# The last unit of a recurrence: low parts by TensorE and ScalarE, last product by VectorE in halves, output product in two parts

## The chip, the cores and the metric

The kernel runs on one core of one Trainium2 chip. The metric is the time of one execution on the device, in microseconds (us); less is better. The core has five engines that each work through a list of their own: TensorE (PE in the rows; its weight loads are PEld), VectorE (DVE), ScalarE (ACT), GpSimd (POOL) and SyncE (SP, which here issues the DMAs). They wait for each other on semaphores only.

## The reference, cut to what matters

Three layers follow each other: a recurrence over the pixels in two directions, causal attention, and a mixture of long convolutions. Cut to what this case touches:

```python
def _mamba_dir(x, ...):                 # once forward (f), once backward (b); x: 4 x 1024 x 64
    xp, z = split(x @ W_in)             # 128 + 128 channels
    xc = silu(xprev * conv_w[:, 0] + xp * conv_w[:, 1] + conv_b)
    dt_r, Bc, Cc = split(xc @ W_x)      # 8, 16, 16
    dt = softplus(dt_r @ W_dt + b_dt)
    def step(h, inp):                   # h: 128 channels x 16 states
        h = exp(dt_t[:, :, None] * A) * h + (dt_t * x_t)[:, :, None] * B_t[:, None, :]
        return h, einsum('bds,bs->bd', h, C_t)
    y = ys + D * xc
    return (y * silu(z)) @ W_out
y = groupnorm_silu(y_f + y_b) + x       # then a layer norm over the 64 channels, and
q, k, v = x @ Wq.T, x @ Wk.T, x @ Wv.T
out = softmax(causal(q @ k.T * 64 ** -0.5)) @ v
```

## The kernel before, in words

The program is three blocks, one after the other, and all engines meet between two blocks: `mamba_stage` (the recurrence), `attention_stage`, `expert_stage` (the convolutions). `mamba_stage` works through eight **units**: four images times two directions. A tile holds the 128 channels on its partitions and the 1024 pixels of an image along them. For each of the 16 **states** s of a unit:

- ScalarE makes the decay exp(dt * A_s) (`decay_of`, L810; three buffers), a few steps ahead of its use.
- VectorE multiplies dt*x by the row B_s, spread over the partitions (`drive_step`, L1008), and runs the scan h = decay * h + drive over the 1024 pixels (`scan_step`, L1025; four buffers `hidden`). For some states GpSimd (L467) or TensorE (L580) makes the drive instead.
- GpSimd multiplies h by the spread row C_s (L477, four buffers `prod`).
- TensorE adds this product to the sum over the states in PSUM (`ps_y`), a matmul with the identity for each half of 512 pixels (`sum_states`, L589). A 32-bit matmul runs as two records, so a sum is four. The sum of state s stands three states later in TensorE's list (`Y_LAG`).

After the last sum of a unit VectorE multiplies by the gate silu(z) (`gate_of`, L1002), and after both directions TensorE applies W_out (`out_product`, L598, four matmuls, eight records) and ScalarE takes the result out of PSUM with its row sums (`norm_take`, L743).

While a unit runs, the engines also prepare the next one. The eighth and last unit has no next one; in its place it prepares attention for the first image (tables `first_attention` of TensorE and VectorE, `last_unit` of ScalarE, keyed by the state after which a step stands): a layer norm, q, k and v. q and k are each kept as a high part, rounded to a shorter 32-bit format (fp32r), and a low part, the rest. Before the change ScalarE copies the high part out of PSUM (L858, L865) and VectorE subtracts it from PSUM to get the low part (`split_q` L1049, `split_k` L1055). All of these share one PSUM tile, `ps_w`, so each step waits for the one ahead: `keys` for `q_ready`, `values` for `k_ready`.

```python
for k in range(2 * N - Y_LAG, 2 * N):                    # L707, TensorE, after its last state
    sum_states(2 * N * (B - 1) + k, k)
    if k == 2 * N - Y_LAG:
        values()
out_product(B - 1)
...
gate_of(u, 1, B)                                         # L1110, VectorE, after its last scan
take_values()
```

The order on each engine is that in which the code is written; nothing reorders it.

Of the kernel before, what the change touches and what calls it, by code (L numbers as in the profile page):

```python
# [192 lines left out]
TOKEN_NORM = 4  # L193


def mamba_stage(nc, ins, a, g, e, x1):
# [6 lines left out]
    with ExitStack() as ctx:  # L203
# [3 lines left out]
        def sem(name):  # L207
# [31 lines left out]
        minus_ident = sb("minus_ident", [128, 128])  # L239
# [25 lines left out]
            dtx_turned dtx_t_ready drive_t_ready drive_turned tok_psum tok_ready ln_step ln_sq ln_rstd xn_ready  # L265
# [7 lines left out]
         tok_psum, tok_ready, ln_step, ln_sq,  # L273
# [67 lines left out]
        with nc.Block() as block:  # L341
# [81 lines left out]
            def _(pool):  # L423
# [81 lines left out]
            def _(pe):  # L505
# [45 lines left out]
                def add_logarithm(u, i):  # L551

                    pe.wait_ge(minus_one_ready, u)
                    add_part(minus_ident, z_raw)
# [28 lines left out]
                def sum_states(n, k, seeded=None):  # L583
# [7 lines left out]
                    mm.then_inc(prod_summed, 1)  # L591

# [81 lines left out]
                def queries():  # L674
                    pe.wait_ge(a.weights_in, ATTENTION_LOADS)
                    pe.wait_ge(xnt_ready, 1)
# [14 lines left out]
                first_attention = {3: tokens, 7: normed, 10: queries, 12: keys}  # L691
# [15 lines left out]
                for k in range(2 * N - Y_LAG, 2 * N):  # L707
                    sum_states(2 * N * (B - 1) + k, k)
                    if k == 2 * N - Y_LAG:
                        values()  # L710
                out_product(B - 1)

            @block.scalar
            def _(act):
# [24 lines left out]
                def norm_take(b):  # L739
# [3 lines left out]
                    nc.scalar.activation(mixed[:, :], ps_y[0:C, :], ACT.Copy, accum_out=g.sums[:, 0:1]).then_inc(g.mixed_ready, 1)  # L743
# [80 lines left out]
                def square():  # L824
                    act.wait_ge(ln_step, 2)
                    nc.scalar.activation(sq, cen, ACT.Square).then_inc(ln_sq, 1)
# [7 lines left out]
                def last_unit(u, i, s):  # L834
# [21 lines left out]
                    if s == 11:  # L856
                        act.wait_ge(q_psum, 1)
                        nc.scalar.activation(a.q_parts[:, :], ps_w[:, :], ACT.Copy,  # L858
                                             scale=float(C) ** -0.5).then_inc(q_high_ready, 1)
                    if s == 12:  # L860
                        act.wait_ge(q_high_ready, 1)
# [1387 lines left out]
```

## Time and profile before

| | us |
|---|---|
| runs of the kernel | 916.76, 919.76, 920.62 (median 919.76) |
| the profiled execution | 924.74 |
| its span (first to last instruction) | 923.0 |
| TensorE busy | 823.8 (89% of the span) |
| VectorE busy | 676.3 (73%) |
| ScalarE busy | 589.2 (64%) |
| GpSimd busy | 539.8 (58%) |

The granted TensorE clock is 0.957 of full speed over the span. Busy shares are means over three blocks with different limits, so they tell little of a single place; what counts is which wait ends last there. Times in the rows are counted from the start of the span.

### The profile page before, as it was taken

What the parts mean: (1) busy time and instruction counts of PE and PEld (TensorE: products, weight loads), DVE (VectorE), ACT (ScalarE), POOL (GpSimd) and SP (SyncE); (2) the same over time, 40 slices, a digit from 0 to 9 for tenths busy, and PEclk for the clock granted to TensorE, in tenths of its full rate; (3) what the DMA queues carried; (4) which work ended last, traced back from release to release, by engine and by line L of the source; (5) the groups of instructions that cost most, each with busy time, mean ns of one, the idle gap of its engine ahead of it and who ended that gap; (6) DMA issues with size and microseconds to landing.
All of it is one profiled execution on the core that took longest, in us unless ns stands there. A gap on an engine that the chain in (4) does not pass through costs nothing. (4 is left out here: it accounts for less than half of the span.)

```text
span 923.0 us, 10941 instructions
## 1 busy us (share of the span) xinstructions
PE 823.8 (89%) x3234; PEld 506.9 (55%) x3234; DVE 676.3 (73%) x742; ACT 589.2 (64%) x937; POOL 539.8 (58%) x368
## 2 busy tenths in 40 slices
PE   4597999889998898977868899989999999999997
PEld 1343443334443343433334555557888888888886
DVE  3889999998989799899943455646565665565665
ACT  4887779678786878876416456556555554555554
POOL 4788989889898798888846944312212221212220
PEclk8699999979999899998997999999999999999999
DMA  6978795878849688695619600002343443343432
GB/s 149 337 254 312 276 320 211 340 284 271 312 189 366 259 275 307 237 347 196 216 13 157 131 1 1 1 1 76 108 137 100 128 121 108 92 130 98 137 105 77
DMA packets 72470, 165.67 MB, mean 179 GB/s; under 512 B 24194, under 2 KB 25236, under 8 KB 72420
## 3 DMA queue, kind: packets, MB, share of 16 engines
q1 hardware_dynamic: 72436, 165.27, 55.7%
q8 instruction: 15, 0.25, 0.1%
q14 instruction: 19, 0.16, 0.1%
HBM read 162.99 MB, written 2.26 MB: 179 GB/s over the span
## 5 line engine op out<-in xcount | busy, mean ns | idle before, releaser
L477 POOL TENSOR_TENSOR prod<-hidden,c_wide 128x1024 f32<-128x1024 f32 x128 | 300.6, 2360 | 51.6 <-DVE hidden L1025 42.7
L589 PE MATMUL ps_y<-prod,ident 128*128 128x512 f32 x512 | 243.4, 616 | 28.1 <-POOL prod L477 15.0
L1025 DVE TENSOR_TENSOR_SCAN hidden<-decay,ps_d 128x1024 f32<-128x1024 f32 x97 | 221.4, 2282 | 12.6 <-ACT decay L810 3.4
L2061 PE MATMUL ps_conv<-hankel,u_high 128*128 128x512 f32 (+1 forms) x768 | 212.5, 358 | 0.1
L589 PEld LDWEIGHTS ps_y<-prod,ident 128*128 128x128 f32 x512 | 95.3, 194 | 149.0 <-issue 122.6
L2061 PEld LDWEIGHTS ps_conv<-hankel,u_high 128*128 128x128 f32 x768 | 138.5, 189 | 24.7 <-DVE u_t L1924 0.3
L2061 PE MATMUL ps_conv<-hankel,u_low 128*128 128x512 f32 (+1 forms) x384 | 137.2, 357 | 0.0
L1889 POOL CAST block_mix<-even 128x256 fp32r (+1 forms) x32 | 12.7, 398 | 204.6 <-PE sums L1930 204.6
L2178 DVE TENSOR_TENSOR stack<-ps_conv,stack 64x512 fp32r<-64x512 f32 x128 | 88.3, 690 | 60.2 <-ACT stack L2145 57.7
L2178 DVE TENSOR_TENSOR qk<-ps_conv,qk 64x512 fp32r<-64x512 f32 x128 | 88.2, 689 | 48.3 <-ACT qk L2145 45.7
L2145 ACT ACTIVATE stack<-ps_conv 64x512 fp32r<-64x512 f32 x128 | 76.2, 595 | 72.3 <-PE ps_conv L2061 70.4
L2145 ACT ACTIVATE qk<-ps_conv 64x512 fp32r<-64x512 f32 x128 | 76.1, 595 | 61.2 <-PE ps_conv L2061 59.1
L1008 DVE TENSOR_TENSOR ps_d<-ps_x,b_wide 128x1024 f32<-128x1024 f32 x73 | 89.9, 1232 | 10.2 <-DMA b_wide<-bc_rows 5.9
L467 POOL TENSOR_TENSOR drive<-dtx,b_wide 128x1024 f32<-128x1024 f32 x31 | 73.5, 2372 | 19.9 <-DMA b_wide<-bc_rows 19.9
L2061 PEld LDWEIGHTS ps_conv<-hankel,u_low 128*128 128x128 f32 x384 | 72.2, 188 | 12.7
L803 ACT ACTIVATE drive_t<-dtx_t,b_t 128x128 f32<-128x128 f32 x192 | 58.6, 390 | 2.1 <-PE ps_d L580 1.9
L1025 DVE TENSOR_TENSOR_SCAN hidden<-ps_w,drive 128x1024 f32<-128x1024 f32 x24 | 54.6, 2274 | 6.6 <-ACT ps_w L816 6.5
L810 ACT ACTIVATE decay<-dt_b,a_neg_b 128x1024 f32<-128x1024 f32 x49 | 53.7, 1138 | 6.6 <-DVE hidden L1025 6.3
L810 ACT ACTIVATE decay<-dt_f,a_neg_f 128x1024 f32<-128x1024 f32 x48 | 52.3, 1138 | 1.3 <-DVE dt_f L985 0.9
L1610 DVE TENSOR_REDUCE max_parts<-sums 128x1 f32<-128x512 f32 (+1 forms) x48 | 27.5, 599 | 28.2 <-PE sums L1285 18.2
L580 PE MATMUL ps_d<-ident,drive_t 128*128 128x128 f32 x192 | 28.0, 288 | 18.8 <-DVE hidden L1025 14.4
L580 PEld LDWEIGHTS ps_d<-ident,drive_t 128*128 128x128 f32 x192 | 23.0, 147 | 34.6 <-DVE hidden L1025 17.2
(285 smaller groups left out, 1186.7 us busy)
## 6 DMA issues: line engine op xcount, KB each, us to landing
c_wide<-bc_rows SPq DMA_DIRECT2D x128, 512.0 KB, 4.9
b_wide<-bc_rows SPq DMA_DIRECT2D x104, 512.0 KB, 5.8
hankel<-filters SPq DMA_DIRECT2D x32, 1026.0 KB, 5.3
plus<-in_M_phi_plus SPq DMA_DIRECT2D x2, 1024.0 KB, 13.8
minus<-in_M_phi_minus SPq DMA_DIRECT2D x2, 1024.0 KB, 17.4
x_pair<-in_x SPq DMA_DIRECT2D x2, 768.0 KB, 9.2
bc_rows<-mixed_and_low SPq DMA_DIRECT2D x8, 128.0 KB, 5.3
out<-plus SPq DMA_DIRECT2D x8, 128.0 KB, 3.6
```

What stands on the lines that cost most here:

```text
L467: nc.gpsimd.tensor_tensor(drive[DRIVE_OF[s]][:, :], dtx[:, :], b_wide[slot][:, :], ALU.mult).then_inc(share_ready, 1)
L477: nc.gpsimd.tensor_tensor(prod[k % PAIR][:, :], hidden[k % DEEP][:, :], c_wide[s % BC_DEEP][:, :], ALU.mult).then_inc(prod_ready, 1)
L580: mm = nc.tensor.transpose(ps_d[:, t * 128:(t + 1) * 128], drive_t[:, t, :], ident[:, :])
L589: mm = nc.tensor.matmul(out, ident[:, :], halves(prod[k % PAIR])[h], start=False, stop=True, skip_group_check=True)
L803: part = nc.scalar.activation(drive_t[:, t, :], dtx_t[:, t, :], ACT.Copy, scale=b_t[:, t, s:s + 1])
L810: nc.scalar.activation(decay[decay_slot(s, last)][:, :], dt[i][:, :], ACT.Exp, scale=a_neg[i][:, s:s + 1]).then_inc(decay_ready, 1)
L1008: nc.vector.tensor_tensor(ps_d[:, :], ps_x[:, :], b_wide[slot][:, :], ALU.mult).then_inc(drive_ready, 1)
L1025: nc.vector.tensor_tensor_scan(hidden[k % DEEP][:, order], left[:, order], right[:, order], 0.0, ALU.mult, ALU.add).then_inc(hidden_ready, 1)
L1610: nc.vector.tensor_reduce(max_parts[:, i, at // H:at // H + 1], ps_s[c % 2][:, 0:n], AX.X, ALU.max, negate=True).then_inc(part_ready, 1)
L2061: mm = nc.tensor.matmul(out, pairs[q][wp][:, 2 * delta + source, :], rows, start=(delta == 0 and term == 0), stop=(delta == 2 * half + 1 a ...
L2145: nc.scalar.activation(stacks[slot][0:C, source, b, :, half * 2 * HEAD:(half + 1) * 2 * HEAD], ps_conv[source][lanes(b), half, :, :], ACT. ...
L2178: nc.vector.tensor_tensor(low, ps_conv[source][lanes(b), half, :, :], high.bitcast(F32), ALU.subtract).then_inc(conv_low, 1)
```

## The change

In the last unit only, besides two lines of the attention block that follow from it:

- **Low parts.** After `queries` and after `keys` TensorE adds minus the high part to `ps_w` with a matmul by `minus_ident` (`take_away`), and ScalarE copies what is left as the low part. VectorE's `split_q` and `split_k` go. The factor 1/8 of q is put on `wq` once, in the first unit, in place of on each copy of q.
- **v.** `values` stands after state 15 in TensorE's list, and ScalarE takes v out of PSUM in place of VectorE.
- **The last product** (state 15) is made by VectorE in two halves in place of by GpSimd whole; TensorE sums each half for itself, and VectorE gates each half for itself.
- **The output product** goes to `ps_w` in place of `ps_y`, direction f ahead of the sum of state 14, direction b after the gate's halves.

```diff
+                            if last and k == 2 * N - 1:
+                                break
                             pool.wait_ge(hidden_ready, n + 1)
...
+                def last_sum(h):
+                    pe.wait_ge(last_prod, h + 1)
+                    nc.tensor.matmul(halves(ps_y)[h], ident[:, :], halves(prod[(2 * N - 1) % PAIR])[h], start=False,
+                                     stop=True, skip_group_check=True).then_inc(prod_summed, 1)
+
+                def last_out(i):
+
+                    if i == 0:
+                        pe.wait_ge(v_ready, 1)
+                    for h, out in enumerate(halves(ps_w)):
+                        pe.wait_ge(gated_ready, 2 * B - 1 + (h + 1 if i else 0))
+                        mm = nc.tensor.matmul(out[0:C, :], w_out[i], halves(gated[i])[h], start=(i == 0), stop=(i == 1),
+                                              skip_group_check=True)
+                    if i:
+                        mm.then_inc(out_ready, 1)
...
+                def take_away(high, done):
+                    for h, out in enumerate(halves(ps_w)):
+                        mm = nc.tensor.matmul(out, minus_ident[:, :], halves(high)[h], start=False, stop=True,
+                                              skip_group_check=True)
+                    mm.then_inc(done, 1)
+
+                def queries_rest():
+                    pe.wait_ge(q_high_ready, 1)
+                    take_away(a.q_parts, q_psum)
...
+                def keys_rest():
+                    pe.wait_ge(k_high_ready, 1)
+                    take_away(a.k_high, k_psum)
...
-                first_attention = {3: tokens, 7: normed, 10: queries, 12: keys}
+                first_attention = {3: tokens, 7: normed, 10: queries, 11: queries_rest, 12: keys, 13: keys_rest, 15: values}
...
-                for k in range(2 * N - Y_LAG, 2 * N):
+                for k in range(2 * N - Y_LAG, 2 * N - 1):
+                    if k == 2 * N - 2:
+                        last_out(0)
                     sum_states(2 * N * (B - 1) + k, k)
-                    if k == 2 * N - Y_LAG:
-                        values()
-                out_product(B - 1)
+                for h in range(2):
+                    last_sum(h)
+                last_out(1)
...
                     if s == 11:
                         act.wait_ge(q_psum, 1)
-                        nc.scalar.activation(a.q_parts[:, :], ps_w[:, :], ACT.Copy,
-                                             scale=float(C) ** -0.5).then_inc(q_high_ready, 1)
+                        nc.scalar.activation(a.q_parts[:, :], ps_w[:, :], ACT.Copy).then_inc(q_high_ready, 1)
+                        act.wait_ge(q_psum, 2)
+                        nc.scalar.activation(a.q_parts[C:, :], ps_w[C:, :], ACT.Copy).then_inc(q_ready, 1)
...
                     if s == 14:
                         act.wait_ge(k_psum, 1)
                         nc.scalar.activation(a.k_high[:, :], ps_w[:, :], ACT.Copy).then_inc(k_high_ready, 1)
+                        act.wait_ge(k_psum, 2)
+                        nc.scalar.activation(a.k_low[:, :], ps_w[:, :], ACT.Copy).then_inc(k_ready, 1)
                     if s == 15:
                         act.wait_ge(k_ready, 1)
                         nc.scalar.activation(a.k_one[0:C, :], a.k_low[0:C, :].bitcast(F32), ACT.Copy).then_inc(k_high_ready, 1)
+                        act.wait_ge(v_psum, 1)
+                        nc.scalar.activation(a.v_one[:, :, 0:C], ps_w[:, 0:H].rearrange("p (i c) -> p i c", i=TILES),
+                                             ACT.Copy).then_inc(v_ready, 1)
...
-                norm_take(B - 1)
+                norm_take(B - 1, ps_w)
...
+                def last_product():
+                    dve.wait_ge(hidden_ready, 2 * B * N)
+                    dve.wait_ge(c_in[(N - 1) % BC_DEEP], 16 * (2 * B * N // BC_DEEP))
+                    dve.wait_ge(prod_summed, 2 * B * N - PAIR)
+                    for h in range(2):
+                        nc.vector.tensor_tensor(halves(prod[(2 * N - 1) % PAIR])[h], halves(hidden[(2 * N - 1) % DEEP])[h],
+                                                halves(c_wide[(N - 1) % BC_DEEP])[h], ALU.mult).then_inc(last_prod, 1)
+
+                def last_gate():
+                    dve.wait_ge(gate_ready, 2 * B)
+                    for h in range(2):
+                        dve.wait_ge(prod_summed, 2 * B * N + h)
+                        nc.vector.tensor_tensor(halves(gated[1])[h], halves(ps_y)[h], halves(gate[1])[h],
+                                                ALU.mult).then_inc(gated_ready, 1)
+
+                first_attention = {3: center_x, 4: spread_x}
...
                 batch(B - 1, last=True)
-                u = 2 * B - 1
-                gate_of(u, 1, B)
-                take_values()
+                last_product()
+                last_gate()
```

**TensorE, from `queries` of the last unit to the end of the block, before.** The sums of states 8 to 15 are the rows with `prod_0` to `prod_3`, twice over:

```order
L670 MATMUL ps_w<-z_raw,wq 128x512 x2
L589 MATMUL ps_y<-prod_0,ident 128x512 x2
L589 MATMUL ps_y<-prod_1,ident 128x512 x2
L670 MATMUL ps_w<-z_raw,wk 128x512 x2
L589 MATMUL ps_y<-prod_2,ident 128x512 x2
L589 MATMUL ps_y<-prod_3,ident 128x512 x2
L589 MATMUL ps_y<-prod_0,ident 128x512 x2
L589 MATMUL ps_y<-prod_1,ident 128x512 x2
L687 MATMUL ps_w<-wv,z_raw 128x64 x8
L589 MATMUL ps_y<-prod_2,ident 128x512 x2
L589 MATMUL ps_y<-prod_3,ident 128x512 x2
L598 MATMUL ps_y<-gated_f,packed_inner_f 64x512
```

Three more rows of L598 follow. **The same stretch of TensorE now,** from the sum of state 9 on (`queries`, the sum of state 8 and the first L701, which takes the high part of q away, stand ahead of it):

```order
L591 MATMUL ps_y<-prod_1,ident 128x512 x2
L688 MATMUL ps_w<-z_raw,wk 128x512 x2
L591 MATMUL ps_y<-prod_2,ident 128x512 x2
L701 MATMUL ps_w<-qk,minus_ident 128x512 x2
L591 MATMUL ps_y<-prod_3,ident 128x512 x2
L591 MATMUL ps_y<-prod_0,ident 128x512 x2
L720 MATMUL ps_w<-wv,z_raw 128x64 x8
L591 MATMUL ps_y<-prod_1,ident 128x512 x2
L606 MATMUL ps_w<-gated_f,packed_inner_f 64x512 x2
L591 MATMUL ps_y<-prod_2,ident 128x512 x2
L597 MATMUL ps_y<-prod_3,ident 128x512 x2
L606 MATMUL ps_w<-gated_b,packed_inner_b 64x512 x2
```

`values` (L687, now L720) stands ahead of the sum of state 13 in place of behind it, and half of the output product (L606) ahead of the sum of state 14.

**VectorE, the end of its list in the block, before:**

```order
L1025 SCALAR_TENSOR_TENSOR hidden_2<-decay_2,ps_d 128x1024
L1055 TENSOR_TENSOR k_low<-ps_w,qk 128x1024
L1008 TENSOR_TENSOR ps_d<-ps_x,b_wide_2 128x1024
L1025 SCALAR_TENSOR_TENSOR hidden_3<-decay_0,ps_d 128x1024
L1002 TENSOR_TENSOR gated_b<-ps_y,gate_b 128x1024
L1060 COPY late<-ps_w 128x8x64
```

and now:

```order
L1067 SCALAR_TENSOR_TENSOR hidden_2<-decay_2,ps_d 128x1024
L1050 TENSOR_TENSOR ps_d<-ps_x,b_wide_2 128x1024
L1067 SCALAR_TENSOR_TENSOR hidden_3<-decay_0,ps_d 128x1024
L1094 TENSOR_TENSOR prod_3<-hidden_3,c_wide_3 128x512 x2
L1101 TENSOR_TENSOR gated_b<-ps_y,gate_b 128x512 x2
```

The subtraction for k and the copy of v are gone, and four halves stand where the gate stood.

## Rows read from the trace of the kernel before

**Rows 1.** The chain that ended last: its second piece (start, us, what):

```profile
624.93 1.08 PE ps_conv L1910 x8
```

**Rows 2.** Busy time in a stretch: TensorE, loads, VectorE, ScalarE, GpSimd; granted clock, DMA:

```profile
464.00:475.00 11.00, 6.01 (x14) 1.85 (x14) 1.82 (x2) 1.42 (x3) 2.58 (x2) 1.00 0.00 0
```

**Rows 3.** VectorE in order of time, states 12 to 15 (start, us, what):

```profile
446.88 1.23 DVE L1049 SCALAR_TENSOR_TENSOR qk<-ps_w,qk 64x1024 fp32r<-64x1024 f32 x1
448.14 1.23 DVE L1008 TENSOR_TENSOR ps_d<-ps_x,b_wide 128x1024 f32<-128x1024 f32 x1
449.50 2.29 DVE L1025 TENSOR_TENSOR_SCAN hidden<-decay,ps_d 128x1024 f32<-128x1024 f32 x1
...
459.08 1.20 DVE L1055 TENSOR_TENSOR k_low<-ps_w,qk 128x1024 fp32r<-128x1024 f32 x1
...
461.55 2.29 DVE L1025 TENSOR_TENSOR_SCAN hidden<-decay,ps_d 128x1024 f32<-128x1024 f32 x1
468.33 1.23 DVE L1002 TENSOR_TENSOR gated_b<-ps_y,gate_b 128x1024 f32<-128x1024 f32 x1 [4.50 <-PE ps_y L589]
```

**Rows 4.** GpSimd in order of time: products of states 9 to 11, 12, 15:

```profile
444.29 7.00 POOL L477 TENSOR_TENSOR prod<-hidden,c_wide 128x1024 f32<-128x1024 f32 x3
...
451.87 2.37 POOL L477 TENSOR_TENSOR prod<-hidden,c_wide 128x1024 f32<-128x1024 f32 x1 [0.53 <-DVE hidden L1025]
...
463.92 2.34 POOL L477 TENSOR_TENSOR prod<-hidden,c_wide 128x1024 f32<-128x1024 f32 x1 [2.32 <-DVE hidden L1025]
```

**Rows 5.** TensorE in order of time, from the sum of state 9:

```profile
446.70 1.98 PE L589 MATMUL ps_y<-prod,ident 128*128 128x512 f32 x4 [0.73 <-POOL prod L477]
448.61 1.98 PE L670 MATMUL ps_w<-z_raw,wk 64*128 64x512 f32 x4
450.52 5.75 PE L589 MATMUL ps_y<-prod,ident 128*128 128x512 f32 x12
...
460.33 2.00 PE L687 MATMUL ps_w<-wv,z_raw 64*128 64x64 f32 x16 [0.39 <-DVE k_low L1055]
462.26 1.98 PE L589 MATMUL ps_y<-prod,ident 128*128 128x512 f32 x4
466.31 1.98 PE L589 MATMUL ps_y<-prod,ident 128*128 128x512 f32 x4 [2.07 <-POOL prod L477]
469.61 1.07 PE L598 MATMUL ps_y<-gated_f,packed_inner_f 128*64 128x512 f32 x2 [1.32 <-DVE gated_b L1002]
...
472.24 1.02 PE L598 MATMUL ps_y<-gated_b,packed_inner_b 128*64 128x512 f32 x2
```

**Rows 6.** ScalarE in order of time: high part of q, decays of states 14 and 15, last output:

```profile
444.31 1.00 ACT L858 ACTIVATE qk<-ps_w 128x1024 fp32r<-128x1024 f32 x1
446.94 1.15 ACT L810 ACTIVATE decay<-dt_b,a_neg_b 128x1024 f32<-128x1024 f32 x1 [1.63 <-DVE hidden L1025]
...
451.88 1.15 ACT L810 ACTIVATE decay<-dt_b,a_neg_b 128x1024 f32<-128x1024 f32 x1 [2.85 <-DVE hidden L1025]
...
473.30 1.02 ACT L743 ACTIVATE mixed_and_low<-ps_y 64x1024 f32<-64x1024 f32 x1 [11.93 <-PE ps_y L598]
```

**Rows 7.** Groups by line and shape, whole span (busy us, mean ns, idle before):

```profile
L2061 PE MATMUL ps_conv<-hankel,u_high 128*128 128x512 f32 x512 | 181.9, 396 | 0.1
L1584 DVE TENSOR_TENSOR u_low<-u_all,u_high 128x512 fp32r<-128x512 f32 x4 | 2.7, 687 | 6.7 <-ACT u_high L1443 6.7
L821 ACT ACTIVATE late<-ps_w 128x512 f32<-128x512 f32 x1 | 0.6, 597 | 2.3 <-PE ps_w L656 2.3
```

**Rows 8.** VectorE and GpSimd in order of time where both read two SBUF tiles:

```profile
420.12 0.86 DVE L1037 SCALAR_TENSOR_TENSOR soft<-small,late 128x512 f32<-128x512 f32 x1
...
420.38 2.82 POOL L467 TENSOR_TENSOR drive<-dtx,b_wide 128x1024 f32<-128x1024 f32 x1
```

**Rows 9.** Busy time in two stretches of the attention block, columns as in group 2:

```profile
482.00:492.00 10.00, 7.25 (x25) 5.42 (x26) 5.09 (x18) 5.06 (x13) 6.16 (x6) 0.50 1.17 141
...
503.00:522.00 19.00, 17.01 (x87) 10.60 (x85) 9.73 (x29) 6.55 (x13) 18.37 (x10) 1.00 1.06 192
```

More of the change, by code:

```diff
@@ L190, in norm_silu @@
                          bias=g.gn[:, 5:6]).then_inc(g.act_ready, 1)
-TOKEN_NORM = 4
+TOKEN_NORM = 5
 def mamba_stage(nc, ins, a, g, e, x1):
@@ L238, in mamba_stage @@
         b_t = sb("b_t", [128, TILES, N])
-        minus_ident = sb("minus_ident", [128, 128])
+        minus_ident = sb("minus_ident", [128, 128], F32R)
         one_plus = a.late[:, 0:L]
@@ L272, in mamba_stage @@
          dtx_turned, dtx_t_ready, drive_t_ready, drive_turned,
-         tok_psum, tok_ready, ln_step, ln_sq,
+         tok_psum, tok_ready, ln_step, last_prod,
          ln_rstd, xn_ready, xnt_psum, xnt_ready, q_psum, q_high_ready, q_ready, k_psum, k_high_ready,
@@ L553, in add_logarithm @@
                     pe.wait_ge(minus_one_ready, u)
-                    add_part(minus_ident, z_raw)
+                    add_part(minus_ident.bitcast(F32), z_raw)
                     pe.wait_ge(ln_ready, u + 1)
@@ L675, in queries @@
                     pe.wait_ge(a.weights_in, ATTENTION_LOADS)
+                    pe.wait_ge(a.idents, 3)
                     pe.wait_ge(xnt_ready, 1)
@@ L737, in silu_gate, with norm_take @@
                     nc.scalar.activation(gate[i][:, :], z_raw[:, :], ACT.Silu).then_inc(gate_ready, 1)
-                def norm_take(b):
+                def norm_take(b, out=ps_y):
                     act.wait_ge(out_ready, b + 1)
@@ L742, in norm_take @@
                     at_least(act, g.rows_out, 16 * b)
-                    nc.scalar.activation(mixed[:, :], ps_y[0:C, :], ACT.Copy, accum_out=g.sums[:, 0:1]).then_inc(g.mixed_ready, 1)
+                    nc.scalar.activation(mixed[:, :], out[0:C, :], ACT.Copy, accum_out=g.sums[:, 0:1]).then_inc(g.mixed_ready, 1)
                 def take_low(u, i):
@@ L825, in square @@
                     act.wait_ge(ln_step, 2)
-                    nc.scalar.activation(sq, cen, ACT.Square).then_inc(ln_sq, 1)
+                    nc.scalar.activation(sq, cen, ACT.Square).then_inc(ln_step, 1)
                 def norm_x():
@@ L933, in batch @@
                                     nc.scalar.activation(a.ident_bf[:, :], ident[:, :], ACT.Copy).then_inc(a.idents, 1)
+                                    act.wait_ge(a.weights_in, ATTENTION_LOADS)
+                                    nc.scalar.activation(a.wq[:, :, :], a.wq[:, :, :], ACT.Copy, scale=float(C) ** -0.5).then_inc(a.idents, 1)
                             if s == 14:
@@ L1040, in spread_x @@
                 def spread_x():
-                    dve.wait_ge(ln_sq, 1)
+                    dve.wait_ge(ln_step, 3)
                     nc.vector.tensor_reduce(a.small[:, 1, :], sq, AX.X, ALU.add).then_inc(ln_step, 1)
-                    dve.wait_ge(ln_step, 3)
+                    dve.wait_ge(ln_step, 4)
                     nc.vector.tensor_scalar(a.small[:, 1, :], a.small[:, 1, :], 1.0 / C, LN_EPS,
                                             ALU.mult, ALU.add).then_inc(ln_step, 1)
-                def split_q():
-                    dve.wait_ge(q_high_ready, 1)
-                    nc.vector.scalar_tensor_tensor(out=a.q_parts[C:, :], in0=ps_w[C:, :], scalar=float(C) ** -0.5,
-                                                   in1=a.q_parts[C:, :].bitcast(F32), op0=ALU.mult,
-                                                   op1=ALU.subtract).then_inc(q_ready, 1)
@@ L1454, in take_q @@
                     nc.scalar.activation(q_parts[b % 2].rearrange("p (h n) -> p h n", h=2), ps_p[:, :, :],
-                                         ACT.Copy, scale=float(C) ** -0.5).then_inc(q_high_ready, 1)
+                                         ACT.Copy).then_inc(q_high_ready, 1)
                     act.wait_ge(q_high_ready, b)
@@ L1588, in split_q @@
                     dve.wait_ge(q_high_ready, b)
-                    nc.vector.scalar_tensor_tensor(out=q_parts[b % 2][C:, :].rearrange("p (h n) -> p h n", h=2),
-                                                   in0=ps_p[C:, :, :], scalar=float(C) ** -0.5,
-                                                   in1=q_parts[b % 2][C:, :].bitcast(F32).rearrange("p (h n) -> p h n", h=2),
-                                                   op0=ALU.mult, op1=ALU.subtract).then_inc(q_ready, 1)
+                    nc.vector.tensor_tensor(q_parts[b % 2][C:, :].rearrange("p (h n) -> p h n", h=2), ps_p[C:, :, :],
+                                            q_parts[b % 2][C:, :].bitcast(F32).rearrange("p (h n) -> p h n", h=2),
+                                            ALU.subtract).then_inc(q_ready, 1)
                 def split_k(b):
```

12 lines of the change are left out of this document (1 added, 11 removed).

## The prediction

> **What bounds the kernel now.** I read the chain of waits first. It begins at 624.93 us, with the block of the convolutions [rows 1], and holds nothing of the recurrence, so it only says that what comes before moves that block as a whole: the three blocks meet at barriers, and whatever the first one ends earlier, the other two start earlier. So I went to the order of time around the end of the first block. The barrier there waits for ScalarE's last copy, which starts at 473.30 [rows 6]. The windows show why this end is dear: in the last 11 us TensorE is busy 6.0, VectorE 1.8, ScalarE 1.4, GpSimd 2.6 [rows 2]. Nobody is full; the engines wait for each other in one line.
>
> That line, step by step: the scan of state 15 ends at 461.55 + 2.29 = 463.84 [rows 3]; GpSimd's product runs from 463.92 to 466.26 [rows 4]; its sum on TensorE from 466.31 to 468.29 [rows 5]; the gate from 468.33 to 469.56 [rows 3]; the output product from 469.61 to 472.24 + 1.02 = 473.26 [rows 5]; then ScalarE's copy [rows 6]. From the end of the scan to that copy: 9.46 us. The scan itself comes late because VectorE's list holds the two subtractions: from 446.88 to 448.14 (1.26), and between the scans of states 14 and 15 another 1.0: drive 1.23, scan 2.29 and gaps make 3.69 a state, and the scans of states 12 and 15 start 12.05 apart, which is 3 x 3.69 + 0.98 [rows 3].
>
> **The change, part by part.**
>
> *The subtractions leave VectorE.* The last scan could end 1.26 + 0.98 = 2.24 earlier, at 461.6. Its other inputs allow it: the decays of states 14 and 15 are ready some 7 and 6 us ahead of need even with a copy of 1.0 us more in front of each (decay of 14: 446.94 before, about 447.7 now, needed at 455.6; decay of 15: released by the scan of state 12, which now ends at 450.54; needed at 459.3) [rows 3, 6]. The products of states 9 to 11 are made back to back until 451.29 [rows 4], ahead of the scans that reuse their inputs.
>
> *The last product on VectorE.* Two halves of 0.69 each (a product of two 128x512 SBUF tiles [rows 7]) in place of 2.34. With the scan at 461.6 the halves are ready at 462.3 and 463.0. Here one row speaks against the change: where VectorE and GpSimd both read two SBUF tiles, VectorE's instruction took 0.86 and GpSimd's 2.82 [rows 8], against 0.69 [rows 7] and 2.37 [rows 4] alone. I take 0.69, since GpSimd's last product (state 14) now ends near 460.4, before the halves start; the upper bound is 0.86 each, 0.3 in all. The Trainium skill, GPSIMD Engine Reference, section 1 (Specifications), says that GpSimd shares its SBUF interfaces with VectorE and that an instruction of VectorE with two SBUF inputs contends for them. By that rule the halves would slow if they met a product, and the trace agrees where they meet.
>
> *Sum, gate and output in halves.* Behind the product only one half of each stays in line: half a sum is about 1.1 (two of four records; four take 1.98), half a gate 0.69, half of one direction's output product 1.07 [rows 5, 7].
>
> *What TensorE's list makes of it.* This decides. From 446.70 on TensorE has hardly a gap left, so I walk its new list. A group of four 32-bit records takes 1.91 to the next one (446.70, 448.61, 450.52 [rows 5]), less where nothing is waited for (three sums in 5.75). The sum of state 9 starts at 446.70 as before, released by GpSimd. `keys` at 448.6: q's low part is there in time (its high copy ends at 445.31 [rows 6], the two short matmuls behind the sum of state 8 by about 446.6, a copy of 1.0 by 447.6). The sum of state 10 at 450.5. Then TensorE waits for the high part of k: ScalarE has the decay of state 15 ahead of it, 450.6 to 451.7, and copies until 452.7 (1.15 and 1.00, the copy as that of q [rows 6]). Each take-away is two matmuls on short-format operands; bounds are 0.4 (one record's 396 ns, fully overlapped) and 0.8 (both in turn) [rows 7]; I take 0.7: 452.8 to 453.5. Sums of states 11 and 12: 453.5, 455.2. `values`, whose 1.93 is the step from 460.33 to 462.26 [rows 5]: 457.1. Sum of state 13: 459.0. Half of the output product (direction f), 1.9: 460.9; v's copy (0.60 [rows 7]) is done at 459.7, so it holds nothing. Sum of state 14: 462.9. Halves of the last sum: 464.7 and 465.7, ending at 465.8 and 466.8; VectorE's halves waited 2 us for their turn. Gates end at 466.5 and 467.5. Second half of the output product: 467.5 to 468.6. ScalarE's copy at 468.6 in place of 473.30: **4.7 us less.**
>
> The new bound is thus TensorE's list and not VectorE's: of the 2.24 us of earlier scans most is spent waiting for it. Even if the scan ended at 463.84 as before, the halves would be ready at 464.5 and 465.2 and the end would move by less than 0.3. What the subtractions' going buys is that `values` no longer waits until 460.33.
>
> *Costed at nothing.* The scaling of `wq` in the first unit (a small copy on ScalarE, whose inputs are there long before); the plain subtraction in place of the scaled one in the attention block, same size; the dropped factor on copies. If that cover were gone, each costs under 0.3 us, once.
>
> **Sum.** The profiled execution took 924.74; the same sum gives 920.0 for it. It was 0.5% above the median of the runs, 919.76, and the change is a fixed shift of one place, so I forecast 919.76 - 4.7 = **915.1**. If every group goes at 1.7 and the take-aways at 0.4, it is 1.5 to 2 better; if each of the new hand-offs costs 0.2 more, 1 worse. This case's own range is 913.3 to 916.2.
>
> **Rivals.**
>
> 1. *VectorE stays the bound.* TensorE catches up before the halves are ready. Then from 461.6: second half of the product 463.0, its sum 464.1, gate 464.8, output 466.0. Gain 7.3, time 912.5. For it: groups without a wait go at 1.7; against it: TensorE would have to save 2 us of a list whose group times stand in the rows.
> 2. *The hand-offs between TensorE and ScalarE hold TensorE's list.* Four new waits stand in it; each microsecond that the high part of k or the low part of q is late goes through to the end, as nothing behind has slack. With 2 us lost, 917.1. Against it: q's low part has a microsecond to spare and k's wait is counted.
> 3. *TensorE's clock falls less.* In the attention block it stood at 0.50, that is 1.2 GHz, from 482 to 492; TensorE was busy 7.25 us in it [rows 9], and work at half speed that runs at 2.4 GHz takes half, 3.6 less. Together with my 4.7: 911.5.
> 4. *TensorE's clock falls once more, and the end is on the other side.* The change moves every start of the next block by 4.7 us against whatever decides the clock. Between 503 and 522 TensorE is busy 17.01 of 19 us at full clock [rows 9]. One more stretch of 10 us at 0.50 there does only half its work, and costs 5.0: 919.76 - 4.7 + 5.0 = 920.1, slower than before. It decides from 9.4 us of additional low clock over busy TensorE on. For it: the three runs of one unchanged kernel lie 3.9 apart. Against it: TensorE's gaps in that block keep their lengths.
>
> The Trainium skill, TensorE: Matmul & The Clock Gate, section "What's actually happening", says that the window in which activity is judged runs free of the program, so that the same work may find the clock in another state. By that rule rivals 3 and 4 can each come about with no change of the gaps; the scatter of the three runs agrees with it, and no run here shows its cause.
>
> **How the numbers follow.** My case 0.62; rival 1 0.12; rival 2 0.06; rival 3 0.08; rival 4 and worse 0.12. A measurement of this kernel tells about 0.5% from no change, which is 4.6 us: the bound lies at 915.2, in the middle of my case. So faster: half of 0.62, 0.12 and 0.08, together 0.52. Slower by over 0.5% takes two more low stretches, 0.03. The same: 0.45. The range reaches from rival 3 up to 919.0: left out are half of rival 3 and rival 4, under 0.2.
>
> **What would show it.** In the profile after: ScalarE's last copy near 468.6; no gap of over 1 us on TensorE between 447 and 467 besides the one ahead of the second take-away; VectorE idle about 2 us or more between the halves of the product and of the gate (rival 1: none on TensorE's account); the scan of state 15 ending near 461.6; `values` near 457. My prediction is wrong if the scan ends no earlier (another input holds it), if a take-away starts over 1 us after the copy that it needs, or if the next two blocks come out with a different length.

## The result, and the profile after

| | before | changed |
|---|---|---|
| median of the first comparison, us | 919.17 (6 runs) | 913.46 (6 runs, 911.35 to 915.95) |
| ratio, 95% interval | | 0.994 [0.9916, 0.9963] |
| profiled execution, its span | 924.74, 923.0 | 911.70, 909.9 |
| scan of state 11 to ScalarE's last copy, from the traces | 28.74 | 23.78 |

The changed kernel is 0.6% faster, and a second comparison further below gives the same. The two profiled executions lie 13.1 us apart in span, more than twice the difference of the medians, so the traces have to be read by stretches and not as wholes. I use one stretch for every run: it begins with VectorE's scan of state 11 in the last unit, the last one that no subtraction has touched, and ends with the start of ScalarE's last copy, which closes the block. It is 28.74 - 23.78 = 4.96 us shorter (forecast: 4.7). What the other 8 us are comes at the end of the section on the experiments.

The chain of waits has not changed in kind (start, us, what):

```profile
611.90 1.08 PE ps_conv L1949 x8
```

TensorE in order of time in the changed kernel, from the sum of state 9, to be held against [rows 5] (start, us, engine, line, operation; in brackets the idle time before it and who ended it):

```profile
441.23 1.98 PE L591 MATMUL ps_y<-prod,ident 128*128 128x512 f32 x4 [0.26 <-POOL prod L479]
443.15 1.98 PE L688 MATMUL ps_w<-z_raw,wk 64*128 64x512 f32 x4
445.06 1.98 PE L591 MATMUL ps_y<-prod,ident 128*128 128x512 f32 x4
447.38 0.74 PE L701 MATMUL ps_w<-qk,minus_ident 128*128 128x512 f32 x2 [0.34 <-ACT qk L900]
447.95 3.60 PE L591 MATMUL ps_y<-prod,ident 128*128 128x512 f32 x8
451.48 2.00 PE L720 MATMUL ps_w<-wv,z_raw 64*128 64x64 f32 x16
453.41 1.98 PE L591 MATMUL ps_y<-prod,ident 128*128 128x512 f32 x4
455.32 1.93 PE L606 MATMUL ps_w<-gated_f,packed_inner_f 128*64 128x512 f32 x4
457.18 1.98 PE L591 MATMUL ps_y<-prod,ident 128*128 128x512 f32 x4
459.00 1.88 PE L597 MATMUL ps_y<-prod,ident 128*128 128x512 f32 x4
460.88 1.93 PE L606 MATMUL ps_w<-gated_b,packed_inner_b 128*64 128x512 f32 x4
```

From the second take-away (L701) on, no row has a bracket: TensorE has no wait until the block ends that a row would show. Before, the sum of state 15 and the output product each waited, 2.07 and 1.32 us [rows 5]. VectorE in the same stretch, against [rows 3]:

```profile
453.81 2.29 DVE L1067 TENSOR_TENSOR_SCAN hidden<-decay,ps_d 128x1024 f32<-128x1024 f32 x1
456.13 1.29 DVE L1094 TENSOR_TENSOR prod<-hidden,c_wide 128x512 f32<-128x512 f32 x2
460.13 1.48 DVE L1101 TENSOR_TENSOR gated_b<-ps_y,gate_b 128x512 f32<-128x512 f32 x2 [2.71 <-PE ps_y L597]
```

The halves of the last product are ready at 457.42, TensorE comes to them at 459.00, and VectorE sits idle 2.71 us ahead of its first gate. ScalarE, against [rows 6]:

```profile
445.13 1.15 ACT L845 ACTIVATE decay<-dt_b,a_neg_b 128x1024 f32<-128x1024 f32 x1 [0.98 <-DVE hidden L1067]
446.30 1.02 ACT L900 ACTIVATE qk<-ps_w 128x1024 fp32r<-128x1024 f32 x1
448.15 1.02 ACT L902 ACTIVATE k_low<-ps_w 128x1024 fp32r<-128x1024 f32 x1 [0.83 <-PE ps_w L701]
462.84 1.02 ACT L778 ACTIVATE mixed_and_low<-ps_w 64x1024 f32<-64x1024 f32 x1 [8.73 <-PE ps_w L606]
```

And the window that ends with the block, against [rows 2]: TensorE is busy 9.39 of 11 us, where it was 6.01.

```profile
453.80:464.80 11.00, 9.39 (x24) 3.15 (x22) 4.96 (x5) 1.98 (x4) 1.56 (x2) 1.00 0.00 0
```

### The profile page after: what moved, and what is told of

It reads as the page before. It is cut to its first block and busy times, and to the rows that moved or that the text cites. A ratio compares the mean times of both kernels' runs of the same rounds, so it can differ in the third digit from the quotient of the medians.

```text
span 909.9 us, 10954 instructions
## 1 busy us (share of the span) xinstructions
PE 823.3 (90%) x3238; PEld 505.1 (56%) x3238; DVE 677.8 (74%) x742; ACT 591.7 (65%) x941; POOL 536.5 (59%) x367
## 5 line engine op out<-in xcount | busy, mean ns | idle before, releaser
L591 PE MATMUL ps_y<-prod,ident 128*128 128x512 f32 x508 | 239.6, 612 | 21.7 <-ACT ps_y L766 12.1
L2100 PEld LDWEIGHTS ps_conv<-hankel,u_high 128*128 128x128 f32 x768 | 138.5, 189 | 24.7 <-DVE u_t L1963 0.3
```

Source lines behind the costliest of these rows:

```text
L591: mm = nc.tensor.matmul(out, ident[:, :], halves(prod[k % PAIR])[h], start=False, stop=True, skip_group_check=True)
L2100: mm = nc.tensor.matmul(out, pairs[q][wp][:, 2 * delta + source, :], rows, start=(delta == 0 and term == 0), stop=(delta == 2 * half + 1 a ...
```

## The experiments

My theory: after the change TensorE's list is the bound of the stretch, and the line from the last scan is not. The rivals: VectorE's list still bounds, or the gain comes from another part than I think. The first eight expectations count from TensorE's sum of state 9 (26.60 before, 21.61 changed). That start moves by up to 0.2 against the scan, and by 0.5 with the second part alone, where the rows merge the sums of states 8 and 9 and the start is read from the single records. So the tables below give what was measured both ways. Each run has one trace; in the two kernels that were traced twice the stretch came out the same to 0.01 (23.78 and 23.78, 27.47 and 27.46). "Gain" is against 28.74.

### Each part alone

**First part alone** (low parts and v by TensorE and ScalarE; the end of the block as before):

```diff
-                            if last and k == 2 * N - 1:
-                                break
...
-                for k in range(2 * N - Y_LAG, 2 * N - 1):
-                    if k == 2 * N - 2:
-                        last_out(0)
+                for k in range(2 * N - Y_LAG, 2 * N):
                     sum_states(2 * N * (B - 1) + k, k)
-                for h in range(2):
-                    last_sum(h)
-                last_out(1)
+                out_product(B - 1)
...
-                norm_take(B - 1, ps_w)
+                norm_take(B - 1)
...
-                last_product()
-                last_gate()
+                gate_of(2 * B - 1, 1, B)
```

> The change's first part alone: low parts by TensorE and ScalarE, v by ScalarE; last product whole on GpSimd, gate whole, output product after it, as before. I read one stretch in every run: from the start of TensorE's sum of state 9 to the start of ScalarE's last copy in the block; it is 26.60 us in the kernel before and 21.61 in the changed one. My theory (VectorE's scans end 2.2 earlier, and the old line from the scan to the copy, 9.46, hangs on them): 24.4. Rival (the new waits between TensorE and ScalarE eat what VectorE saves): 26 or more.

**Second part alone** (tail in halves; subtractions on VectorE after states 11 and 14, `values` behind the sum of state 13):

```diff
-                first_attention = {3: tokens, 7: normed, 10: queries, 11: queries_rest, 12: keys, 13: keys_rest, 15: values}
+                first_attention = {3: tokens, 7: normed, 10: queries, 12: keys}
...
                     sum_states(2 * N * (B - 1) + k, k)
+                    if k == 2 * N - Y_LAG:
+                        values()
...
-                        act.wait_ge(q_psum, 2)
-                        nc.scalar.activation(a.q_parts[C:, :], ps_w[C:, :], ACT.Copy).then_inc(q_ready, 1)
...
-                        act.wait_ge(k_psum, 2)
-                        nc.scalar.activation(a.k_low[:, :], ps_w[:, :], ACT.Copy).then_inc(k_ready, 1)
...
-                first_attention = {3: center_x, 4: spread_x}
+                first_attention = {3: center_x, 4: spread_x, 11: split_q, 14: split_k}
```

> The second part alone: last product, sum, gate and output in halves, direction f early, v by ScalarE; but both subtractions are on VectorE as before and the matmul for v stands behind the sum of state 13. My theory (from the matmul for v on, TensorE works without a gap through v, half of the output product, the sum of state 14 and the last halves): the stretch is 23.9. Rival (the line from the last scan bounds it: scan end 17.14 and 4.5 after it): 21.7.

> The kernel with the second part alone once more: in its first run TensorE's clock fell to half inside the stretch. I now read from the start of VectorE's scan of state 11 to ScalarE's last copy, which is 28.74 in the kernel before, 23.78 in the changed one, 26.49 with the first part alone. My theory with TensorE's clock full: 26.0 (2.7 less than before). If the tail in halves is worth no more than the first run's 27.47 says: 27.5 again at full clock.

| | from sum of state 9 | from scan of state 11 | gain |
|---|---|---|---|
| first part alone | 24.32 | 26.49 | 2.25 |
| second part alone | 25.88 and 25.81 | 27.47 and 27.46 | 1.27 and 1.28 |
| both (the change) | 21.61 | 23.78 | 4.96 |

The first part alone gives what the two subtractions took from the scans, to the hundredth: the scan of state 15 starts 14.74 after that of state 11 in place of 16.99. The second part alone gave less than either theory had (25.9 in place of 23.9 or 21.7, counted from the sum of state 9). The rows of its second run (TensorE in order of time) show where:

```profile
458.19 2.00 PE L720 MATMUL ps_w<-wv,z_raw 64*128 64x64 f32 x16 [0.39 <-DVE k_low L1110]
460.88 3.42 PE L606 MATMUL ps_w<-gated_f,packed_inner_f 128*64 128x512 f32 x4 [0.69 <-ACT late L906]
464.22 1.98 PE L591 MATMUL ps_y<-prod,ident 128*128 128x512 f32 x4
```

Half of the output product took 3.42 in place of 1.93, and the windows around it give the clock (columns as in [rows 2]; the last three numbers are granted clock, DMA share and GB/s):

```profile
455.00:460.00 5.00, 3.79 (x20) 2.48 (x20) 4.87 (x4) 1.06 (x1) 3.12 (x2) 1.00 0.00 0
460.00:464.00 4.00, 3.31 (x6) 0.80 (x5) 2.99 (x3) 0.60 (x1) 0.00 (x0) 0.57 0.00 0
464.00:470.00 6.00, 5.85 (x13) 1.89 (x12) 1.38 (x2) 0.12 (x1) 0.00 (x0) 1.00 0.00 0
```

The clock stood at half, 1.2 GHz, for about 3.4 us (0.57 over 4 us), and did so at the same place in both runs of this kernel, 18.1 us behind the start of the scan of state 11; my second expectation had counted on a run without it. Taking off 3.42 - 1.93 = 1.49 gives 25.97, and a gain of 2.77 (forecast 26.0), but no run shows that. The first theory, "without a gap", had also left out the wait of 0.69 for ScalarE's copy of v. So of 4.96 us, 2.25 are the first part's, 1.27 the second's, and 1.44 come only with both. That this last piece is the low clock, which the changed kernel does not show there, is worked out from its size and not shown by itself.

### Inside the tail

**The last product whole on GpSimd:**

```diff
-                            if last and k == 2 * N - 1:
-                                break
...
-                    pe.wait_ge(last_prod, h + 1)
+                    pe.wait_ge(prod_ready, 2 * B * N)
...
-                last_product()
                 last_gate()
```

> The changed kernel with the last product whole on GpSimd as before; each half of the sum waits for the whole of it. My theory (TensorE's list is the bound; the product would be ready about 0.5 us before TensorE reaches it): the stretch stays 21.6. Rival (it is the shorter product that brings the end forward): 1.0 to 1.7 longer, 22.6 to 23.3.

**The last gate whole:**

```diff
-                        pe.wait_ge(gated_ready, 2 * B - 1 + (h + 1 if i else 0))
+                        pe.wait_ge(gated_ready, 2 * B - 1 + i)
...
-                    for h in range(2):
-                        dve.wait_ge(prod_summed, 2 * B * N + h)
-                        nc.vector.tensor_tensor(halves(gated[1])[h], halves(ps_y)[h], halves(gate[1])[h],
-                                                ALU.mult).then_inc(gated_ready, 1)
+                    dve.wait_ge(prod_summed, 2 * B * N + 1)
+                    nc.vector.tensor_tensor(gated[1][:, :], ps_y[:, :], gate[1][:, :], ALU.mult).then_inc(gated_ready, 1)
```

> The changed kernel with the last gate as one instruction of 1024 after both halves of the last sum. My theory (the gate stands in line after TensorE's list and has no cover when whole): gate 1.23 after the sum, then 1.93 of output product: 1.3 longer, 22.9. Rival (halves of VectorE's work pay a fixed part each, so whole is no worse): 21.6 or less.

**Direction f of the output product behind the last sums:**

```diff
-                    if k == 2 * N - 2:
-                        last_out(0)
...
                     last_sum(h)
+                last_out(0)
                 last_out(1)
```

> The changed kernel with direction f of the output product moved behind the last halves of the sum, so that both directions stand at the end. The stretch from TensorE's sum of state 9 to ScalarE's last copy is 21.61 us in the changed kernel. My theory (TensorE's list is full, so the same work in another order takes as long; at the end it covers the gate): 21.6 to 21.8. Rival (what is done early is saved at the end): 1.9 longer, 23.5.

| | from sum of state 9 | from scan of state 11 | gain | VectorE idle before its last gate |
|---|---|---|---|---|
| the change | 21.61 | 23.78 | 4.96 | 2.71 |
| product whole on GpSimd | 21.78 | 23.78 | 4.96 | 4.03 |
| gate whole | 23.02 | 25.17 | 3.57 | 3.57 |
| direction f last | 21.26 | 23.42 | 5.32 | 0.68 |

The shorter last product is worth nothing here. GpSimd's and TensorE's rows of that run:

```profile
462.34 2.35 POOL L477 TENSOR_TENSOR prod<-hidden,c_wide 128x1024 f32<-128x1024 f32 x1 [1.33 <-DVE hidden L1065]
```

```profile
463.34 1.99 PE L589 MATMUL ps_y<-prod,ident 128*128 128x512 f32 x4
465.17 1.88 PE L595 MATMUL ps_y<-prod,ident 128*128 128x512 f32 x4
```

The product is there at 464.69, and TensorE comes to it at 465.17 with no wait. The gate in halves is worth 1.39. As a whole it leaves TensorE idle for that long, between the last sum and the output product:

```profile
464.64 1.88 PE L597 MATMUL ps_y<-prod,ident 128*128 128x512 f32 x4
467.91 1.93 PE L606 MATMUL ps_w<-gated_b,packed_inner_b 128*64 128x512 f32 x4 [1.39 <-DVE gated_b L1100]
```

Direction f done early is worth less than nothing: moved back to the end it covers the gates just as well, and the stretch is 0.36 shorter. The rows show its two halves of the output product 1.77 apart, with the last sums ahead of them:

```profile
457.91 1.92 PE L597 MATMUL ps_y<-prod,ident 128*128 128x512 f32 x4
459.76 1.93 PE L606 MATMUL ps_w<-gated_f,packed_inner_f 128*64 128x512 f32 x4
461.53 1.88 PE L606 MATMUL ps_w<-gated_b,packed_inner_b 128*64 128x512 f32 x4
```

The single records, which the rows merge, show where the 0.36 comes from. Inside a group they start 0.43 apart. Where TensorE goes from a sum to the output product or back, the steps there are together 0.14 to 0.21 longer, three times in the changed kernel (0.54) and once here (0.14); two sums in a row, or the two directions in a row, cost 0.04 or nothing. What makes such a turn dearer no run isolates. My forecast was 0.0 to 0.2 longer; the sign was wrong, and the theory behind it (order does not matter on a full list) holds only to these turns.

### Load on VectorE, load off TensorE

**Two products more on VectorE** (after states 11 and 14, result unused):

```diff
+                def pad():
+                    dve.wait_ge(skip_ready, 2 * B)
+                    nc.vector.tensor_tensor(xc[:, :], ps_x[:, :], dt[0][:, :], ALU.mult).then_inc(ln_step, 1)
+
-                first_attention = {3: center_x, 4: spread_x}
+                first_attention = {3: center_x, 4: spread_x, 11: pad, 14: pad}
```

> The changed kernel with two more products of 1024 on VectorE where the two subtractions stood (after the scans of states 11 and 14; their result is used nowhere). The last scan ends 2.4 us later. My theory (TensorE's list is the bound, VectorE waits some 2 us for it): the stretch grows by 0.3 to 0.6, to 22.0. Rival (VectorE's list is the bound): by 2.4, to 24.0.

**One sum and two sums of TensorE left out** (state 12, in the second run 12 and 13, n in (124, 125); all but 32 columns of each, so the output lacks these states' share of the last unit):

```diff
+                    if isinstance(n, int) and n in (124,):
+                        nc.tensor.matmul(ps_y[:, 0:32], ident[:, :], prod[k % PAIR][:, 0:32], start=False, stop=True,
+                                         skip_group_check=True).then_inc(prod_summed, 1)
+                        return
```

> The changed kernel, but TensorE's sum of state 12 in the last unit is left out but for its first 32 columns. My theory: TensorE's list loses 1.7 us in front of the last halves, and the end comes as much earlier: 19.9. Rival (VectorE's list or the line from the last scan is the bound): 21.6.

> As the run with one sum less, but the sums of states 12 and 13 are both left out but for 32 columns. My theory: now the halves of the last product and the product of state 14 bound the end: 19.4, only 0.5 less than with one sum left out, and VectorE no longer waits for TensorE before its first gate by more than half a sum, 1.1. If TensorE's list were still all that counts: 18.2.

| | from sum of state 9 | from scan of state 11 | against the change | VectorE idle before its last gate |
|---|---|---|---|---|
| two products more on VectorE | 22.62 | 24.76 | +0.98 | 1.71 |
| one sum less on TensorE | 20.05 | 22.20 | -1.58 | 1.12 |
| two sums less on TensorE | 19.77 | 21.76 | -2.02 | 0.69 |

With one sum left out, the step from the sum of state 11 to `values` is 1.95 us, where it was 451.48 - 447.95 = 3.53 for two sums:

```profile
449.62 1.88 PE L595 MATMUL ps_y<-prod,ident 128*128 128x512 f32 x4
451.33 0.30 PE L591 MATMUL ps_y<-prod,ident 128*128 128x32 f32 x2
451.57 2.00 PE L724 MATMUL ps_w<-wv,z_raw 64*128 64x64 f32 x16
```

So TensorE's list became 1.58 shorter (the 32 columns that stay take the rest of the 1.7), and the stretch became 1.58 shorter: all of it comes through. Leaving out the next sum gives only 0.44 more, as other releases come last then. In the run with two sums less, TensorE's rows name two of them:

```profile
453.96 1.93 PE L610 MATMUL ps_w<-gated_f,packed_inner_f 128*64 128x512 f32 x4 [0.35 <-ACT late L911]
456.27 1.98 PE L595 MATMUL ps_y<-prod,ident 128*128 128x512 f32 x4 [0.38 <-POOL prod L479]
```

The third is VectorE's last product: its first half ends at 458.20, and TensorE starts its sum at 458.26. With 2.02 us less than the change the stretch is thus near the line from the last scan as well.

The load on VectorE did cost more than I had expected: the scan of state 15 starts 1.97 later, and 0.98 comes through. The reason is further back, on VectorE, ScalarE and TensorE (rows of that run):

```profile
446.76 2.29 DVE L1067 TENSOR_TENSOR_SCAN hidden<-decay,ps_d 128x1024 f32<-128x1024 f32 x1
```

```profile
449.14 1.15 ACT L845 ACTIVATE decay<-dt_b,a_neg_b 128x1024 f32<-128x1024 f32 x1 [1.95 <-DVE hidden L1067]
450.32 1.02 ACT L900 ACTIVATE qk<-ps_w 128x1024 fp32r<-128x1024 f32 x1
```

```profile
451.39 0.73 PE L701 MATMUL ps_w<-qk,minus_ident 128*128 128x512 f32 x2 [1.36 <-ACT qk L900]
```

The decay of state 15 waits for the scan of state 12, which starts 4.67 after that of state 11 in place of 3.69; the high part of k stands behind this decay on ScalarE, and the second take-away waits 1.36 in place of 0.34. So VectorE's delay reaches the end through TensorE's list, by a wait in its middle. The sizes agree: the first added product makes the scan of state 12 0.98 late, and 0.98 is what the stretch grows by. The 0.99 that the second one adds behind state 14 is covered; VectorE's idle time ahead of the gate falls from 2.71 to 1.71.

### What follows from it

Two versions put that to use. **The low part of k by VectorE again, after state 13:**

```diff
-                first_attention = {3: tokens, 7: normed, 10: queries, 11: queries_rest, 12: keys, 13: keys_rest, 15: values}
+                first_attention = {3: tokens, 7: normed, 10: queries, 11: queries_rest, 12: keys, 15: values}
...
-                        act.wait_ge(k_psum, 2)
-                        nc.scalar.activation(a.k_low[:, :], ps_w[:, :], ACT.Copy).then_inc(k_ready, 1)
...
-                first_attention = {3: center_x, 4: spread_x}
+                first_attention = {3: center_x, 4: spread_x, 13: split_k}
```

> The changed kernel, but the low part of k is subtracted by VectorE again, now after the scan of state 13, and TensorE's second take-away goes. My theory (TensorE's list is the bound; the take-away and the wait in front of it are 1.0 of it; VectorE has 2.7 to spare and gives 1.1): from the scan of state 11 to the last copy 22.8 in place of 23.78. Rival (VectorE's list bounds once more): 24.0 or more.

**The high part of k ahead of the decay of state 15:**

```diff
-                    own = {0: (3, 4), 1: (5,), 2: (7,), 4: (8,), 7: (10,), 8: (11,), 9: (12,), 10: (13,), 12: (14,), 13: (15,)}
+                    own = {0: (3, 4), 1: (5,), 2: (7,), 4: (8,), 7: (10,), 8: (11,), 9: (12,), 10: (13,), 12: (14,)}
...
                         nc.scalar.activation(a.k_high[:, :], ps_w[:, :], ACT.Copy).then_inc(k_high_ready, 1)
+                        decay_of(u, i, 15, True)
                         act.wait_ge(k_psum, 2)
```

> The changed kernel, but ScalarE copies the high part of k before it makes the decay of state 15, not after. My theory (TensorE's second take-away waits 0.4 for that copy, and all behind it is full): 23.4 in place of 23.78. Rival (such a wait is swallowed by a later one): 23.8.

**The changed kernel once more,** in the same comparison:

> The changed kernel once more, to tell what its place in the last unit gives from what the rest of the program adds. From the scan of state 11 to the last copy: 23.8 again, to 0.1. Whole time against the kernel before: 5.0 less if the rest is scatter of the clock; 6 or more if the change also helps elsewhere.

| | stretch from scan 11 | median, us (runs) | ratio to before, 95% |
|---|---|---|---|
| before | 28.74 | 920.93 (17) | |
| the change again | 23.78 | 914.28 (11) | 0.9937 [0.9914, 0.9960] |
| low part of k by VectorE | 22.75 | 913.25 (7) | 0.9935 [0.9912, 0.9958] |
| high part of k first | 23.15 | 914.14 (4) | 0.9934 [0.9910, 0.9958] |

Both shorten the stretch, the first as forecast (22.8), the second by more (23.4). TensorE's list in the first of them has lost the take-away and the wait ahead of it:

```profile
444.27 5.42 PE L591 MATMUL ps_y<-prod,ident 128*128 128x512 f32 x12
449.62 2.00 PE L720 MATMUL ps_w<-wv,z_raw 64*128 64x64 f32 x16
```

and in the second the take-away (L701) runs right behind the sum, so it overlaps it and saves 0.6 in place of 0.4:

```profile
449.60 1.98 PE L591 MATMUL ps_y<-prod,ident 128*128 128x512 f32 x4
451.02 1.03 PE L701 MATMUL ps_w<-qk,minus_ident 128*128 128x512 f32 x2
451.88 3.60 PE L591 MATMUL ps_y<-prod,ident 128*128 128x512 f32 x8
```

In the whole time neither can be told from the change; 1 us is 0.1%, and the intervals are over 4 us wide. All that is claimed for them is the stretch.

### The rest of the time

The second comparison gives 0.63% or 5.8 us, the first 0.6% or 5.5, the stretch 4.96. The three blocks of all profiles:

| | before | change | change again | all 14 profiles |
|---|---|---|---|---|
| start of the scan of state 11 | 444.56 | 439.06 | 444.22 | 437.99 to 445.49 |
| last copy to the convolutions' first matmuls | 151.63 | 149.06 | 149.29 | 149.06 to 151.63 |
| from there to the end of VectorE's last addition | 294.64 | 294.63 | 294.64 | 294.63 to 294.65 |

The 5.5 us by which the changed kernel's profile was ahead at the scan of state 11 are scatter: its own second profile is at 444.22. That and the 2.6 us of the attention block make up the 8 us that the two profiled executions differ beyond the stretch.

The traces show what the scatter of the first 440 us goes with. Up to the scan of state 11 TensorE's clock stood at half for 54.6 us in the profile before and in the second one of the changed kernel, and for 41.0 us in its first. Over all profiles, those with 37.5 to 47.8 us at half reach that scan at 437.99 to 442.09, those with 51.2 to 58.0 us at 442.42 to 445.49.

The attention block differs by the places of its low stretches and not by their sum, which is 20.5 us in all three profiles of the table. Counted from the last copy, they begin at 8.7, 25.8, 49.7 and 141.8 us before, and at 3.5, 10.4, 27.4 and 140.1 in the changed kernel (4.2, 11.0, 24.7 and 140.7 in its second profile). Two runs on top of the change, one sum less on TensorE and the product whole on GpSimd, happen to have them within 0.3 us of the places before, and there the block takes 151.25 and 150.91, against 151.63. So of the 2.6 us at most 0.4 to 0.7 are left for the change itself, and no run shows that they are its.

Whether the 0.5 to 0.8 us between the stretch and the ratios are anything stays open: the intervals are over 4 us wide, and of the kernel before there is one profile only. My last expectation had two cases for this, 5.0 less or 6 and more; 5.8 by the ratio (6.65 by the medians) decides between neither.

## Why the prediction was right or wrong

- **What bounds the kernel.** Right: the line at the end of the block was where the change counts; the convolutions' block moved as a whole, to 0.02 us. The attention block did not keep its length (2.6 and 2.3 us shorter), which the prediction had named as a sign of being wrong. The sign was too strict: most of that goes with the places of the low clock.
- **The subtractions leave VectorE, 2.24.** The first part alone measured 2.25.
- **The walk through TensorE's new list.** Counted from the sum of state 9, forecast and measured: `keys` 1.9 and 1.92; sum of state 10 3.8 and 3.83; second take-away 6.1 and 6.15; sum of state 11 6.8 and 6.72; `values` 10.4 and 10.25; sum of state 13 12.3 and 12.18; half of the output product 14.2 and 14.09; sum of state 14 16.2 and 15.95; last halves 18.0 and 17.77; copy 21.9 and 21.61. All rows within 0.3. The take-away took 0.57 where I had 0.7, the sums of states 11 and 12 3.53 for 3.6, and the half of the output product 1.86 for 2.0. These three are most of the 0.26 by which 4.7 was short of 4.96.
- **VectorE waits 2 us for TensorE.** 2.71 measured. One sum less made TensorE's list 1.58 shorter and the stretch 1.58 shorter, so the bound is where I put it.
- **"Even if the scan ended at 463.84 the end would move by less than 0.3."** Wrong: 1.97 of delay cost 0.98. I had compared only the ends of the two lists and left out the wait in the middle of TensorE's, on ScalarE's copy of k behind a decay behind a scan. That wait had stood in the walk itself (452.8); the step that failed is to take the subtraction behind state 11 as covered like the one behind state 14. It was the first, with 0.98, that came through. The remark before it, that most of the 2.24 us is spent waiting for TensorE's list, is off for the same reason: of the 1.97 us put back, half came through.
- **The last product in halves.** I priced it at 0.69 a half; each took 0.69, but they start 0.61 apart, so both took 1.29. That it would hide behind TensorE's list I said, and the run with GpSimd's product shows that it is worth 0. The contention with GpSimd did not come up, as GpSimd's last product ended at 454.84 and the halves start at 456.13.
- **Rivals.** Rival 1 (7.3 us) did not come: its limit shows when two sums are left out, 2.02 beyond the change. Rival 2 did not come either: the one wait of 0.34 at the second take-away stood in my walk. Of rivals 3 and 4, the attention block had as much low clock as before, 20.5 us, in other places; the block was 2.6 us shorter in one profile, 2.3 in the next.
- **The number.** 915.1 was forecast, 913.46 and 914.28 measured, inside 911.5 to 919.0; faster by over 0.5% had 0.52, and both ratios lie there, with intervals that reach across that bound. The time before was 919.17 and 920.93 in the two comparisons and not 919.76, so the medians differ by 5.7 and 6.65, and the stretch holds 4.96 of it. That the number came so near is in part luck; the stretch is what the walk foretold.
- **Slips.** The chances for faster add up to 0.51 and not 0.52. The decay of state 15 is ready 7.6 us ahead of need by the prediction's own times and not 6. The scaling of `wq`, costed at nothing, was isolated by no run.

## What to carry to other kernels

When a line of waits between engines is cut into halves and overlapped, the next bound is often the list of the engine that serves all of them; walk its new list row by row, from the first start that the change does not move, and price each group by the distance of starts and not by its busy time. A part of such a change can be worth nothing (here the shorter last product) or a little less than nothing (here the early half of the output product) while the whole pays, and only runs that undo one part at a time show it. Look for waits in the middle of the full list: they let a delay of another engine through that a comparison of the two ends would call hidden.

## What the runs showed that I had not expected

With the tail in halves alone, TensorE's granted clock stood at half for about 3.4 us at the same place in both runs. It fell within the gap of 0.69 behind the matmuls for v, and by the rows it cost 1.5 of a gain that would have been 2.8 us. The kernel before has longer gaps on TensorE in the same stretch, 2.07 and 1.32 [rows 5], at full clock [rows 2]. A gain in one block can thus be given back in part by the clock inside that block, here the same way in both runs, while in the attention block the places of the low clock vary between two profiles of one kernel.
